# A decoder layer on one core: in quads 11 to 14 the term D times u enters the sum through ScalarE and an identity product, and the fillers end at index 13

## The reference

```python
proj = hidden_states @ W_in.T
x, gate = (proj[..., :D_IN], proj[..., D_IN:])
...
x = jax.nn.silu(xc)                      # xc: causal convolution over 4 tokens
ts, Bm, Cm = (ssm[..., :R], ssm[..., R:R + N], ssm[..., R + N:])   # ssm = x @ W_x.T, each normed
dt = jax.nn.softplus(ts @ W_dt.T + b_dt)
def step(state, inp):
    dA = jnp.exp(dt_t[..., None] * A)
    state = state * dA + (dt_t * u_t)[..., None] * B_t[:, None, :]
    y = jnp.einsum('bdn,bn->bd', state, C_t)
y = ys.transpose(1, 0, 2) + x * D        # the term of the change; u is this x
y = y * jax.nn.silu(gate)
return y @ W_out.T
```

## Time and profile before

| | |
|---|---|
| profiled execution, its own time | 2971.96 us |
| its span | 2969.9 us |
| VectorE busy | 2552.7 us, 86% |
| TensorE busy | 2729.3 us, 92% |
| GpSimd busy | 1922.2 us, 65% |
| ScalarE busy | 1695.5 us, 57% |
| quads 11, 12, 13, 14, from one first skip to the next | 121.75, 118.95, 125.31, 118.02 us |

### The profile page before, as it was taken

The page is one execution under the profiler, slowest core; times in us unless marked ns, Lnnn a source line. Parts: engine busy times, 40 slices in busy tenths (PEclk is TensorE's granted clock), DMA queues, the critical chain, the costliest instruction groups (busy, mean ns, idle before and its releaser), DMA issues.

```text
span 2969.9 us, 35293 instructions
## 1 busy us (share of the span) xinstructions
PE 2729.3 (92%) x11120; PEld 1557.2 (52%) x11120; DVE 2552.7 (86%) x3525; ACT 1695.5 (57%) x2848; POOL 1922.2 (65%) x886
## 2 busy tenths in 40 slices
PE   8988899999989999998999887888889999999996
PEld 4444555555555555555555454555544555555553
DVE  2289999999999999999999999999966787787785
ACT  2366556565665657566565654756534555555553
POOL 1179798888969889896988988889731222222221
PEclk9998999999999999999999999889899999999998
DMA  5352333433343343334333333322401211111110
GB/s 173 132 123 72 112 104 95 136 116 110 91 152 105 94 135 120 107 99 144 110 93 97 100 87 94 121 87 65 113 29 38 97 56 56 64 56 56 64 60 26
DMA packets 132876, 281.32 MB, mean 95 GB/s; under 512 B 12528, under 2 KB 12656, under 8 KB 132224
## 3 DMA queue, kind: packets, MB, share of 16 engines
q1 hardware_dynamic: 132736, 279.59, 31.1%
HBM read 245.86 MB, written 33.69 MB: 94 GB/s over the span
## 4 chain that ended last, share of the span: by engine, by line
PE 54%; DVE 32%; issue 8%; ACT 4%; POOL 1%; DMA 0%; DVEq 0%; POOLq 0%; SPq 0%; ACTq 0%
DVE arena L1429 17%; PE banks L524 16%; PE banks L548 9%; DVE arena L1445 7%; PE banks L618 7%; PE banks L764 4%; PE banks L717 4%; PE banks L673 3%; PE banks L698 3%; PE banks L561 2%; PE banks L688 2%; PE banks L728 2%; ACT banks L1166 1%; DVE arena L1376 1%; PE banks L771 1%
## 5 line engine op out<-in xcount | busy, mean ns | idle before, releaser
L1344 POOL TENSOR_TENSOR arena<-arena 128x2048 f32<-128x2048 f32 x255 | 1158.6, 4544 | 78.5 <-PE banks L618 78.5
L1429 DVE TENSOR_TENSOR_SCAN arena<-banks,arena 128x512 f32<-128x512 f32 x1024 | 1184.7, 1202 | 14.9 <-POOL arena L1344 8.9
L1166 ACT ACTIVATE banks<-arena,a_sb 128x508 f32<-128x508 f32 x1024 | 696.8, 684 | 727.9 <-DVE arena L1429 724.2
L524 PE MATMUL banks<-arena 128*128 128x512 f32 x2048 | 954.6, 603 | 11.4 <-DMA arena<-in_xT 8.2
L618 PEld LDWEIGHTS banks<-ident,arena 128*128 128x128 f32 x4096 | 490.4, 145 | 396.7 <-issue 177.4
L618 PE MATMUL banks<-ident,arena 128*128 128x128 f32 x4096 | 572.5, 283 | 115.1 <-DVE arena L1445 64.1
L524 PEld LDWEIGHTS banks<-arena 128*128 128x128 f32 x2048 | 373.0, 195 | 363.1 <-issue 358.8
L1445 DVE SCALAR_TENSOR_TENSOR arena<-banks,cg,arena 128x512 f32<-128x512 f32 x640 | 452.4, 737 | 76.4 <-PE banks L618 75.8
L548 PE MATMUL banks<-arena 128*128 128x512 f32 x1024 | 472.9, 601 | 5.7 <-DMA arena<-in_WoutT 4.4
L1276 POOL TENSOR_TENSOR arena<-arena 128x512 f32<-128x512 f32 x240 | 306.9, 1279 | 207.2 <-ACT arena L910 204.8
L1357 POOL TENSOR_TENSOR arena<-arena 128x512 f32<-128x512 f32 x128 | 141.4, 1104 | 431.9 <-DVE arena L1610 431.8
(11 more groups left out here) (139 smaller groups left out, 2973.3 us busy)
## 6 DMA issues: line engine op xcount, KB each, us to landing
arena<-b_scratch SPq DMA_DIRECT2D x128, 512.0 KB, 5.1
arena<-in_WinX SPq DMA_DIRECT2D x128, 256.0 KB, 2.8
arena<-in_WinZ SPq DMA_DIRECT2D x128, 256.0 KB, 2.7
arena<-in_WoutT SPq DMA_DIRECT2D x32, 1024.0 KB, 5.9
u_scratch<-arena SPq DMA_DIRECT2D x64, 256.0 KB, 5.1
arena<-u_scratch SPq DMA_DIRECT2D x16, 1024.0 KB, 9.5
arena<-x_scratch SPq DMA_DIRECT2D x32, 512.0 KB, 3.4
arena<-in_xT SPq DMA_DIRECT2D x14, 1024.0 KB, 8.2
```

What stands on the lines that cost most here:

```text
L524: last = nc.tensor.matmul(home(kind, i), wr[w % 2][:, k, :], x[:, k, :], start=(k == 0), stop=(k == KC - 1))
L1166: nc.scalar.activation(by_seq(bank(i % 2))[:, :, 1:SEQ], by_seq(dt[s % 2][:, i, :])[:, :, 1:SEQ], ACT.Exp, scale=a_sb[:, QD * q + i, n:n + ...
L1344: nc.gpsimd.tensor_tensor(hb[n % 4].rearrange("p (i t) -> p i t", i=QD), dtu, brep[pair % 3][:, n % 2:n % 2 + 1, :].broadcast_to([P, QD, G ...
L1429: nc.vector.tensor_tensor_scan(h, bank(i % 2), h, 0.0, ALU.mult, ALU.add)\
```

## The change

It applies to quads 11 to 14 (`lean(s)`), and does five things there.

1. ScalarE multiplies u by D in place (`act_skip`, in e = 20, 28, 42, 45), and TensorE puts the result into the four Y banks by a product with the identity (`pe_skip`, 512 columns each), two in index 14 and two in index 15. The turned sums are then joined to it: all five pieces of a Y tile are real products that accumulate, where before three were transposes. VectorE's four skip operations go.
2. The fillers have a list and table of their own (LEAN, LEAN_SIZES): two and two or three per place, without empty places, none in indices 14 and 15.
3. VectorE's additions of the output tiles move to indices 7, 8, 9, 10, 12, 13, 14, 14 (quad 11: 3, 4, 4, 5, 12, 13, 14, 14).
4. ScalarE's work on the gate tile Z3 moves from e = 60 to 62 to e = 52 to 54 (quad 11: 54 to 56).
5. In quad 11 GpSimd's product for Z2 moves from index 14 to 13.

```diff
+LEAN = ["Z0 Z1 D0 D1 Z2 D2 O0 O1 O2 D3 O3 Z3 O4 O5 O6 O7".split(),
+        "Z0 O0 O1 O2 O3 D0 Z1 D1 Z2 D2 D3 Z3 O4 O5 O6 O7".split()]
+LEAN_SIZES = [sum([(2, 2)] + [(2, 3)] * 6 + [(2, 2)] + [(2, 3)] * 6 + [(0, 0)] * 2, ()),
+              sum([(2, 2), (2, 3), (3, 3), (2, 3), (2, 2)] + [(2, 3)] * 8 + [(2, 2)] + [(0, 0)] * 2, ())]
...
+def lean(s):
+
+    return 0 < s < NS - 1 and not has_x(s)
+
+
+def skips(s):
+
+    return QD * sum(not lean(v) for v in range(s))
+
+
 def order(s):
+    if lean(s):
+        return LEAN[s % NQ == NQ - 1]
...
-            sizes = SIZES[s % NQ] if s else (HEAD,) + OPEN
+            sizes = LEAN_SIZES[s % NQ == NQ - 1] if lean(s) else SIZES[s % NQ] if s else (HEAD,) + OPEN
...
+        def pe_skip(pe, s, i):
+
+            pe_room(pe, "Y", QD * s + i)
+            pe.wait_ge(S["ud_ok"], QD * sum(lean(v) for v in range(s)) + i + 1)
+            nc.tensor.matmul(home("Y", QD * s + i), ident[:, :], uq[s % 2][:, i, :], start=True, stop=False)
...
                 turn(0)
                 turn(1)
                 pe_filler(pe, s, 2 * n + past)
+                if lean(s) and n >= N - 2:
+                    pe_skip(pe, s, 2 * (n - N + 2))
...
                 pe_filler(pe, s, 2 * n + 1 + past)
+                if lean(s) and n >= N - 2:
+                    pe_skip(pe, s, 2 * (n - N + 2) + 1)
 
             pe.wait_ge(S["acc_ok"], KEPT * (s + 1))
             pe.wait_ge(S["sum_ok"], (N - 1) * (s + 1))
             pe.wait_ge(S["sum2_ok"], (len(SHARED) - 1) * (s + 1))
             for i in range(QD):
+                y = home("Y", QD * s + i)
+                if lean(s):
+                    for b in range(GB):
+                        last = nc.tensor.matmul(y[:, b * P:(b + 1) * P], acc[:, b, i * P:(i + 1) * P], ident[:, :],
+                                                start=False, stop=(b == OWN))
+                        if b == SPLIT:
+                            last = nc.tensor.matmul(y[:, b * P:(b + 1) * P], acc2[:, i * P:(i + 1) * P],
+                                                    ident[:, :], start=False, stop=False)
+                    last.then_inc(S["yt_mm"], 1)
+                    continue
                 pe_room(pe, "Y", QD * s + i)
-                y = home("Y", QD * s + i)
                 for b in (0, 1, OWN):
                     nc.tensor.transpose(y[:, b * P:(b + 1) * P], acc[:, b, i * P:(i + 1) * P], ident[:, :])
...
+        def act_skip(act, s, i):
+
+            d = QD * (s % NQ) + i
+            act.wait_ge(S["dtu_ok"], s)
+            nc.scalar.activation(uq[s % 2][:, i, :], uq[s % 2][:, i, :], ACT.Copy, scale=dsk[:, d:d + 1])\
+                .then_inc(S["ud_ok"], 1)
...
+            if lean(s) and e in (20, 28, 42, 45):
+                act_skip(act, s, (20, 28, 42, 45).index(e))
...
-            if e == 60:
+            z3 = 60 if not lean(s) else 52 if q < NQ - 1 else 54
+            if e == z3:
                 act_z_copy(act, Z + 3)
-            if e == 61:
+            if e == z3 + 1:
                 act_z_exp(act, Z + 3)
                 act_z_ln(act, Z + 3)
-            if e == 62:
+            if e == z3 + 2:
                 act_z_sig(act, Z + 3)
...
-                if n == (12 if q < NQ - 1 and s > 0 else 14):
+                if n == (12 if q < NQ - 1 and s > 0 else 13 if lean(s) else 14):
...
-                    if n == ((3, 4, 4, 5) if late else (7, 8, 9, 9))[c] if c < 4 else n == (14, 15, 15)[c - 4]:
+                    if n == ((3, 4, 4, 5) if late else (7, 8, 9, 10 if lean(s) else 9))[c] if c < 4 else \
+                            n == ((12, 13, 14) if lean(s) else (14, 15, 15))[c - 4]:
                         dve_out(dve, s, c)
+                if lean(s) and n == 14:
+                    dve_out(dve, s, 7)
...
-            skip(0)
+            if not lean(s):
+                skip(0)
             for i in range(QD):
-                if i < QD - 1:
+                if i < QD - 1 and not lean(s):
                     skip(i + 1)
                 dve.wait_ge(S["z_ok"], QD * s + i + 1)
-                dve.wait_ge(S["fin1"], QD * s + i + 1)
+                if lean(s):
+                    dve.wait_ge(S["yt_mm"], QD * s + i + 1)
+                else:
+                    dve.wait_ge(S["fin1"], skips(s) + i + 1)
                 nc.vector.tensor_tensor(yq[:, i, :], home("Y", QD * s + i), zs[:, i, :], ALU.mult)\
```

More of the change, by code:

```diff
@@ L124 @@
 dt_mm dt_abs dt_exp dt_ln dt_ok dtu_part dtu_ok cg_ok exp_ok bm_part bm_ok scan_ok t_done acc_ok part_ok sum_ok part2_ok sum2_ok yt_mm fin1 fin
-z_mm z_copied z_exp z_ln z_sig z_ok o_mm r_added ln_stats ln_aggr ln_eps ln_rstd ln_shift ln_ok x1_stored
+z_mm z_copied z_exp z_ln z_sig z_ok o_mm r_added ln_stats ln_aggr ln_eps ln_rstd ln_shift ln_ok ud_ok x1_stored
 p2_const wv_loaded ones_set ph_mm ph_ok gs_ok cn_loaded ct_loaded x1_loaded xres_loaded out_stored
@@ L1546, in dve_step @@
                 dve_between(dve, s, n)
-            if s > 0:
+            if s > 0 and not lean(s):
                 dve_out(dve, s, 7)
```

## The result

The changed kernel takes 3014.8 us, the median of four runs (3013.06 to 3017.28), against 2971.3 before (four runs, 2968.34 to 2972.52): a ratio of 1.0149, interval 1.0131 to 1.0166. It is 43.5 us slower. The profiled execution has a span of 3014.8 us, an own time of 3017.28 (before: 2971.96).

A forecast was written before the change was run, and what follows sets the result against it. VectorE was taken to lead where fillers are even, GpSimd's chain to set each quad's end. Terms 1.4 − 7.0 + 30 + 4.5 = +28.9 us on 2971.96 gave 3000.9, stated as 2999 (median), range 2978 to 3020.

The forecast's parts named there:

- stalls of O0, O1, O2, three quads: Quads 12 to 14: O tiles wait on TensorE for inputs, holding up VectorE's turns; 10 us per quad, +30.
- GpSimd in quad 11: Its Z2 product waits for ScalarE's sigmoid, making VectorE's scan 4.1 us late and the quad's end later: +4.5 us.
- the quads' ends: Last sum to last gate product, quads 11 to 14: 6.6 us instead of 6.25; +0.35 per quad, +1.4 in all.
- spread fillers: Quads 11 to 14: even fillers take three quarters of 9.2 us of VectorE's waits for turns: −7.0 us.
- that upper end: Quads' ends with Y at half clock in every quad: +14.4 us, 13 us more than the forecast took.
- The end of −9.8: Most favourable limit of the spread-fillers term in quads 11 to 14: 9.8 us saved; the other limit was 0.
- the same stalls, but the clock holds: Rival: O-tile stalls in quads 12 to 14 occur with TensorE's clock staying up; +14 us, 2985; chance 0.2.
- covered by the one before: Rival: stalls exist, but O1's and O2's are covered by the preceding one; +3.6 us, 2974, no change; chance 0.07.
- the waits cost nothing: Rival: inputs are there when TensorE reaches the O tiles in quads 12 to 14; faster, 2957; chance 0.1.
- The slow one: Rival: clock down at most stalls and at the quad's end; +62 at worst, +45 taken, 3016; chance 0.15.
- my main case: Whole kernel: stalls, quad 11's GpSimd delay, quads' ends and spread fillers sum to +28.9 us, 2999; chance 0.48.

The follow-up runs named there:

- e1: Changed kernel with only filler numbers in quads 12 to 14 altered, so O0, O1 and O2 begin behind turn 1 of indices 6, 7 and 8: 2979.55 us.
- e2: Changed kernel with GpSimd's product for Z2 in quad 11 back at index 14: 3009.78 us.
- f5: Changed kernel with the D2 product, the filler just before O0, issued five times instead of once in quads 12 to 14: 3004.87 us.
- f1_dve_skip: e4_both with VectorE's skips behind the Y tiles in place of the identity products; lists and sizes stay: 2973.61 us.
- e4_both: Changed kernel with the edits of e1 and e2 together: 2975.93 us.
- f3: f2 with one filler instead of three behind the narrow products of index 1 in quad 11: 2967.12 us.
- f2: e4_both with the last identity product issued four times in quads 11 to 14, the first three overwritten: 2968.43 us.
- e3: Changed kernel; in quads 12 to 14 only O0 moved behind turn 1 of index 6, leaving two products instead of three before index 7: 2990.43 us.

## Why the prediction was right, step by step

The forecast was 2999 in a range of 2978 to 3020, the measurement 3014.8. The mechanism and the sign were right, and the total is 16 us too low: 11.7 us in quads 11 to 14, and 4.1 outside them. No two errors cancelled; each of the steps came out at my figure or dearer. The steps against what the traces show:

| step | forecast | measured |
|---|---|---|
| stalls of O0, O1, O2, three quads | +30 | +32.8 of waiting; e1 made the quads 32.9 shorter |
| GpSimd in quad 11 | +4.5 | +4.6 (e2, without the quad's end) |
| the quads' ends | +1.4 | +5.2 |
| spread fillers | −7.0 | about −3.0 |
| sum | +28.9 | +40.6 in these quads by the windows |

**The stalls.** The places, the cause and what stood behind each wait were as forecast; only the split was off. I had 2.5, 3.4 and 1.8 us at full clock and 2.3 more for the clock. O2's wait came out at 1.8. The first wait was 4.2 to 4.7, of which f5 shows that 2.5 is the queue and the rest the clock: the figure at full clock holds (2.54 worked out, 2.51 measured) when the clock is held up. The second wait was 3.37 us in quad 13, where the three products behind it ran at full clock, as worked out, and 5.1 in the two others. TensorE idled 3.63 us before O0 and 3.13 before O1 in quad 12, not over 4. What misled me was the earlier trace rows, where a product ran fast after 3.26 us of idling; here, after 3.63, it ran at half clock.

**GpSimd in quad 11.** The 4.1 us late at the scan that I forecast are 4.12 in the trace. The chain from dt times u to the last sum stayed 25.4 to 25.5 us in all four quads, so the shift went through to the end.

**The quads' ends.** This step was mis-sized. I took 6.6 us per quad, "nearer to full clock since the low stretch need not cover all of Y". It covered two or three of the four tiles, and it was 7.2 to 8.5. With the clock up it is 5.6 to 5.7 (I had 5.4). The rule that I weighed there (the Trainium skill, TensorE: Matmul & The Clock Gate, Part 4: PE-mode transpose: transposes don't bring TensorE to its full clock) is not contradicted by the runs: in f1_dve_skip, with nothing but transposes in indices 14 and 15 of quad 12, the granted clock was 0.62 from 1819.5 to 1831.9, and the last eight transposes took 1.97 us. But TensorE was busy for only 5.20 of these 12.40 us, and in e4_both, with identity products in the same indices, the clock was 0.67 over the last 11.3 us before Y. So no run separates the transposes from the idling. The 13 us extra of that upper end are not reached, since the clock comes up midway through Y (0.56, then 0.96, in quad 12 of the changed kernel).

**Spread fillers.** This step failed by more than half. Outside the new stalls and the quads' ends, VectorE's waits for turns in the first twelve indices were 9.5 us before and are 6.5 now. Two of the old waits went, in quads 12 and 14; in quad 13 four waits (0.99, 1.30, 0.71 and 0.45 us) stand where two were, and in quad 11 three fillers behind the narrow products of index 1 made a wait of 1.23 into one of 2.47. I had scaled quad 12's 2.3 us to four quads, 9.2, which was near; taking three quarters of it away was the guess that failed. The end of −9.8 that I gave is more than the 9.2 that I had to save, and it stands in three of the rivals' sums, each 0.6 us too low by it. f3 shows besides that such a wait need not count in full: 1.7 us less of it made quad 11 only 0.5 us shorter.

The terms measured add up to 32.8 + 4.6 + 5.2 − 3.0 = 39.6, beside the 40.6 of the windows; for 1.0 us I have no term. Of the rivals, "the same stalls, but the clock holds" is refuted by f5 and f2, "covered by the one before" by e3, and "the waits cost nothing" by the trace itself. The slow one, clock down at most stalls and at the end, at 3016, describes the measurement better than my main case did: both the stalls at indices 6 and 7 and the ends ran partly at half clock.

## What to carry over

In an in-order queue, place a piece of work by when its inputs are there, and look at what stands behind it: here three tiles that began two or three products too early cost 11 us per quad, and moving them a few places by a table of numbers gave 33 us in the three quads back. A stall on TensorE has two parts, the wait and the products behind it, which often ran at half clock here, and a stretch without products ahead of a critical burst of them is paid for in the burst; a few products whose result is thrown away can be cheaper than the idling. Taking work off an engine that is waiting for another at that moment, like VectorE at a quad's end, gave nothing here.

## What the runs showed that I had not expected

- Adding 12 products of 0.86 us (10.3 us of TensorE's time) made the changed kernel 9.9 us faster, and adding 12 others made e4_both 7.5 us faster.
- The length of the idling just before does not settle the level. After 1.47 us two products took 3.78 us (e1_later_o), after 3.63 us the same; after 2.57 us one product took 1.13, at full clock, and so did that of the earlier trace rows after 3.26.
- The instructions do not settle it either. O1's three products in quad 13, the same instructions in both kernels, took 2.84 us after 2.96 us of idling in the changed kernel and 4.11 after 2.99 in e2_z14. Y in quad 11, again the same, had a granted clock of 1.00 in e2_z14 and 0.64 in e4_both, after 2.56 and 2.57 us of idling. What decides was not tried. So the size of one stall in one trace can be luck, and a series is needed: of the 28 quad ends in the seven kernels with plain identity products one took 5.61 us and the others 6.94 to 8.56, while all eight with three products more before Y (f2_warm, f3_warm_q11) took 5.60 to 5.69.
